# Expert stage: the weights of both layers as one record per page from HBM, instead of from SBUF by registers on TensorE and VectorE

## What is computed

```python
x = x + xattn(layernorm(x), ctx_1024, Wq, bq, Wk, bk, Wv, bv, Wo, bo)
n = layernorm(x)                                   # 16384 tokens x 256
e = argmax(n @ router_w.T + router_b, axis=-1)     # one of 32
h = relu(n @ weights1[e] + bias1[e])               # 256 -> 64
x = x + relu(h @ weights2[e] + bias2[e])           # 64 -> 256
```

## Time and profile before

| | before |
|---|---|
| median of 3 runs | 1328.94 us |
| profiled execution: span | 1326.5 us |
| profiled execution: what lies around the span | not shown; the median is 2.4 us above the span |
| PE busy / DVE / ACT / POOL | 87% / 71% / 63% / 64% |
| attention stage up to the table's load | about 0 to 1059 us |
| expert stage | 1059 to 1326.5 us |
| DMA in the expert stage (1100 to 1250 us) | share 0.54, 168 to 172 GB/s |

### The profile page before, as it was taken

One profiled execution on the slowest core, in us unless ns is written; L12 is line 12 of the kernel. 1 busy time (PEld: TensorE's weight loads), 2 busy tenths in 40 slices (PEclk: granted clock), 3 DMA queues, 4 the chain that ended last, 5 costly groups with the idle time before them and its releaser, 6 DMA issues.

```text
span 1326.5 us, 38982 instructions
## 1 busy us (share of the span) xinstructions
PE 1149.7 (87%) x15015; PEld 879.9 (66%) x15015; DVE 943.3 (71%) x2449; ACT 833.1 (63%) x1892; POOL 850.8 (64%) x1613
## 2 busy tenths in 40 slices
PE   4899999999999999999999999999986077777785
PEld 3677777777767777777777777777764066666664
DVE  4588788888778878788888778877775155555554
ACT  2577677777677777777777677777764044444443
POOL 4235677677776766777677776766744746666665
PEclk9899999999999999999999999999998589999999
DMA  8215222422222222222222222222101255555540
GB/s 253 89 58 113 66 74 66 131 81 70 73 83 69 66 73 66 66 74 66 67 81 70 73 83 70 66 74 58 34 27 39 92 169 175 169 163 181 161 120 19
DMA packets 89235, 120.37 MB, mean 91 GB/s; under 512 B 12176, under 2 KB 71963, under 8 KB 88861
## 3 DMA queue, kind: packets, MB, share of 16 engines
q1 hardware_dynamic: 75230, 84.03, 22.2%
q0 software_dynamic: 13824, 33.85, 7.0%
HBM read 60.61 MB, written 59.31 MB: 90 GB/s over the span
## 4 chain that ended last, share of the span: by engine, by line
PE 52%; DVE 32%; issue 7%; ACT 4%; POOL 2%; DVEq 1%; DMA 1%; another core or an unknown queue 0%; SPq 0%; POOLq 0%
DVE mx L565 14%; PE pB L787 11%; PE pA L740 9%; PE pB L794 5%; PE sc L747 4%; PE sc L942 4%; DVE tr L589 3%; PE m L950 3%; PE sc L769 3%; DVE nrm L593 3%; PE m L756 3%; DVE row L574 3%; PE sc L933 2%; PE sc L778 2%; PE pA L731 2%
## 5 line engine op out<-in xcount | busy, mean ns | idle before, releaser
L565 DVE TENSOR_REDUCE mx<-m 128x4 bf16<-128x512 f32 x512 | 324.0, 673 | 60.6 <-PE m L756 60.4
L446 ACT ACTIVATE arena<-sc 128x512 f32<-128x512 f32 x512 | 264.5, 604 | 33.9 <-PE sc L778 21.7
L397 POOL DMA_INDIRECT out<-arena x160 | 159.6, 997 | 104.7 <-DVE arena L706 69.0
L769 PE MATMUL sc<-qk 32*128 32x256 f32 x2048 | 167.0, 397 | 0.2
L368 POOL DMA_INDIRECT pages<-row,slot_i x128 | 131.9, 1030 | 49.3 <-issue 32.3
L787 PE MATMUL pB<-arena 128*32 128x128 f32 x4096 | 147.3, 276 | 14.3 <-issue 0.9
L589 DVE STREAM_TRANSPOSE tr<-pB 128x512 f32<-128x512 f32 x128 | 91.8, 717 | 82.6 <-PE pB L787 73.8
L524 ACT ACTIVATE arena<-sc 128x256 f32<-128x256 f32 x160 | 61.2, 383 | 135.4 <-PE sc L933 82.4
L794 PE MATMUL pB<-wo_s,aT 128*128 128x256 f32 x512 | 139.5, 396 | 3.9 <-DVE aT L598 3.9
L787 PEld LDWEIGHTS pB<-arena 128*32 128x32 f32 x4096 | 107.9, 110 | 37.4 <-DVE row L574 31.1
L276 POOL TENSOR_SCALAR row<-row 128x2 f32<-128x2 f32 x64 | 14.6, 228 | 161.4 <-ACT xn L430 161.4
(11 more groups left out here) (133 smaller groups left out, 2716.6 us busy)
## 6 DMA issues: line engine op xcount, KB each, us to landing
arena<-pages SPq DMA_DIRECT2D x40, 520.0 KB
xs<-x_in SPq DMA_DIRECT2D x128, 128.0 KB, 2.1
cT<-ctxT SPq DMA_DIRECT2D x64, 256.0 KB, 4.3
pages<-empty SPq DMA_DIRECT2D x120, 130.0 KB
pages<-empty SPq DMA_DIRECT2D x1, 5200.0 KB, 18.9
out<-arena POOLq DMA_INDIRECT x160
w2s<-w SPq DMA_DIRECT2D x1, 2080.0 KB
qk<-w SPq DMA_DIRECT2D x1, 2064.0 KB
```

Source lines behind the costliest of these rows:

```text
L397: pool.indirect_dma_start(out_rows, bass.IndirectOffsetOnAxis(pr[:, r, COL_TOKEN:COL_TOKEN + 1].bitcast(U32), 0), pr[:, r, 0:D], None, bou ...
L446: act.activation(pt[:, u % 2, g].rearrange("p i k -> p (i k)"), sc[g][:, :], ACT.Exp).then_inc(S["exp_out"], 1)
L565: ins = dve.tensor_reduce(mx[:, 32 * g:32 * g + 4], mb[i][:, :].rearrange("p (h k) -> p h k", h=4), AX.X, ALU.max)
L769: pe.matmul(dst, kT[rows, q % 2, c, u * P:(u + 1) * P], qM[rows, q % 2, :, c, u * P:(u + 1) * P], start=(c == 0), stop=False, skip_group_c ...
```

## The change

Both layers' weights of an expert become one record of 385 used columns (of a pitch of 388) times 128 partitions in a new HBM tensor `weights`: columns 0 to 128 hold the first layer and its bias, columns 129 to 384 the second layer with its bias row. The records are put together by three DMAs of SP in the attention stage, behind quads 5, 6 and 7. In the expert stage SP alone reads `table`, four values at a time, and issues for each page a DMA of 128 rows of 1540 bytes from `weights` at a register's offset into a ring `wt` of 12 (over the space of `qk`). The page loads keep their ring of 20, but each is now issued between the register loads and the weight loads of a group of four, two groups ahead. TensorE waits for the landing of a record (`w_in0` to `w_in11`) and takes both layers from the ring at fixed addresses. VectorE's copy, both engines' register loads, `w1s`, `w2s`, `w1p` and `w1_out` are gone.

```diff
-W1R = 5
-W1C = 192
+WR = 12
+WC = 388
...
+    W1E = 2 * HID + 1
+    W2E = W1E + D
+    weights = nc.dram_tensor("weights", (E, P, WC), F32).ap()
...
-        w2s = sb("w2s", [E, D])
-        w1s = qk[:, 0:E * (2 * HID + 1)].rearrange("p (e h) -> p e h", e=E)
+        wt = qk[:, 0:WR * WC].rearrange("p (n c) -> p n c", c=WC)
-        w1p = cT[:, :, :].rearrange("p c t -> p (c t)")[:, 0:W1R * W1C].rearrange("p (n c) -> p n c", c=W1C)
...
-                if q == 1:
-                    sp.dma_start(w2s[64:P, :, :], empty[64:P, 0:D].unsqueeze(1).to_broadcast([64, E, D])).then_inc(S["w2_zero"], 16)
                 if q == 5:
+                    sp.dma_start(weights.rearrange("e p c -> p e c")[64:P, :, W1E:W2E],
+                                 empty[64:P, 0:D].unsqueeze(1).to_broadcast([64, E, D])).then_inc(S["w2_zero"], 16)
+                if q == 6:
+                    sp.dma_start(weights.rearrange("e p c -> p e c")[:, :, 0:W1E], w1).then_inc(S["ld_w1"], 16)
+                if q == 7:
                     sp.wait_ge(S["w2_zero"], 16)
-                    sp.dma_start(w2s[0:HID + 1, :, :], w2).then_inc(S["ld_w2"], 16)
+                    sp.dma_start(weights.rearrange("e p c -> p e c")[0:HID + 1, :, W1E:W2E], w2).then_inc(S["ld_w2"], 16)
 
             after(sp, "T_done", 16, NQ - 1, 15)
-            sp.dma_start(w1s, w1).then_inc(S["ld_w1"], 16)
+            sp.wait_ge(S["ld_w1"], 16)
+            sp.wait_ge(S["ld_w2"], 16)
...
-            for n in range(0, PAGES, GP):
+
+            def load_pages(n):
                 g = n % RING // GP
                 if n >= RING:
                     sp.wait_ge(S[f"wrote{g}"], n // RING * (16 * GP))
                 sp.dma_start(pr[:, g * GP:(g + 1) * GP, :], page_view[:, n:n + GP, :]).then_inc(S[f"page_in{g}"], 16)
+
+            def load_weights(n, e):
+                if n >= WR:
+                    after(sp, "y_done", 1, n - WR, 0)
+                sp.dma_start(wt[:, n % WR, 0:W2E],
+                             weights[bass.ds(e, 1), :, 0:W2E].rearrange("e p c -> p (e c)")).then_inc(S[f"w_in{n % WR}"], 16)
+
+            load_pages(0)
+            load_pages(GP)
+            sp.wait_ge(S["table_in"], 16)
+            for n in range(0, PAGES, AT_ONCE):
+                _, experts = nc.values_load_multi_w_load_instructions(table[0:1, n:n + AT_ONCE], engines=(mybir.EngineType.SP,), min_val=0, max_val=E - 1)
+                if n + 2 * GP < PAGES:
+                    load_pages(n + 2 * GP)
+                for k in range(AT_ONCE):
+                    load_weights(n + k, experts[k])
...
             def h_copy(n):
                 after(act, "h_done", 1, n, 0)
                 act.activation(hT[0:HID, n % DEEP, :], sc[2 + n % 2][0:HID, 0:P], ACT.Relu,
-                               bias=w1p[0:HID, n % W1R, 2 * HID:2 * HID + 1]).then_inc(S["h_out"], 1)
+                               bias=wt[0:HID, n % WR, 2 * HID:2 * HID + 1]).then_inc(S["h_out"], 1)
...
-                if n >= W1R:
-                    after(dve, "h_out", 1, n - W1R, 0)
-                dve.tensor_copy(w1p[:, n % W1R, 0:2 * HID + 1], w1s[:, bass.ds(e, 1), :].rearrange("p e h -> p (e h)")).then_inc(S["w1_out"], 1)
...
-            after(dve, "ctx_out", 1, NQ - 1, 0)
-            dve.memset(w1p[:, :, 2 * HID + 1:W1C], 0.0)
...
-            dve.wait_ge(S["ld_w1"], 16)
-            dve.wait_ge(S["table_in"], 16)
...
-                        _, experts = nc.values_load_multi_w_load_instructions(table[0:1, n:n + AT_ONCE], engines=(mybir.EngineType.DVE,), min_val=0, max_val=E - 1)
-                    page_norm(n, experts[n % AT_ONCE])
+                    page_norm(n)
...
             def page_first(n):
-                after(pe, "w1_out", 1, n, 0)
+                pe.wait_ge(S[f"w_in{n % WR}"], n // WR * 16 + 16)
...
-                    ins = pe.matmul(sc[2 + n % 2][:, 0:P], w1p[:, n % W1R, i * HID:i * HID + P],
+                    ins = pe.matmul(sc[2 + n % 2][:, 0:P], wt[:, n % WR, i * HID:i * HID + P],
...
-                pe.matmul(mid[n % 4][:, 0:D], hT[:, n % DEEP, :], w2s[:, bass.ds(e, 1), :].rearrange("p e d -> p (e d)"),
+                pe.matmul(mid[n % 4][:, 0:D], hT[:, n % DEEP, :], wt[:, n % WR, W1E:W2E],
...
-            pe.wait_ge(S["ld_w2"], 16)
-            pe.wait_ge(S["table_in"], 16)
...
-                        _, experts = nc.values_load_multi_w_load_instructions(table[0:1, n - 4:n - 4 + AT_ONCE], engines=(mybir.EngineType.PE,), min_val=0, max_val=E - 1)
-                    page_second(n - 4, experts[n % AT_ONCE])
+                    page_second(n - 4)
```

More of the change, by code:

```diff
@@ L152, in build @@
           noff_out step_out fresh_slots all_slots grew_out shift_out nxt_old room_out nxt_out own_slots slot_int
+          w_in0 w_in1 w_in2 w_in3 w_in4 w_in5 w_in6 w_in7 w_in8 w_in9 w_in10 w_in11
           scattered table_in page_in0 page_in1 page_in2 page_in3 page_in4 wrote0 wrote1 wrote2 wrote3 wrote4
-          w1_out pn_out pT_done h_done y_done pT_out h_out po_out""".split()
+          pn_out pT_done h_done y_done pT_out h_out po_out""".split()
         names += [f"ld_x{k}_{u}" for k in range(4) for u in range(QB)]
@@ L689, in _, with page_norm @@
                             scan(s - 2)
-            def page_norm(n, e):
+            def page_norm(n):
                 r = n % RING
-                if n >= W1R:
-                    after(dve, "h_out", 1, n - W1R, 0)
-                dve.tensor_copy(w1p[:, n % W1R, 0:2 * HID + 1], w1s[:, bass.ds(e, 1), :].rearrange("p e h -> p (e h)")).then_inc(S["w1_out"], 1)
                 if r % GP == 0:
@@ L708, in _ @@
             mid = [mb[0], mb[1], pA, pB]
-            after(dve, "ctx_out", 1, NQ - 1, 0)
-            dve.memset(w1p[:, :, 2 * HID + 1:W1C], 0.0)
             dve.tensor_copy(hT[64:P, :, :].rearrange("p n t -> p (n t)"),
                             cst[64:P, C_ONE:C_ONE + 1].to_broadcast([64, DEEP * P])).then_inc(S["ex_init"], 1)
-            dve.wait_ge(S["ld_w1"], 16)
-            dve.wait_ge(S["table_in"], 16)
             for n in range(PAGES + LAG):
                 if n < PAGES:
-                    if n % AT_ONCE == 0:
-                        _, experts = nc.values_load_multi_w_load_instructions(table[0:1, n:n + AT_ONCE], engines=(mybir.EngineType.DVE,), min_val=0, max_val=E - 1)
-                    page_norm(n, experts[n % AT_ONCE])
+                    page_norm(n)
                 if n >= LAG:
@@ L941, in page_first, with page_second @@
                 for i in range(2):
-                    ins = pe.matmul(sc[2 + n % 2][:, 0:P], w1p[:, n % W1R, i * HID:i * HID + P],
+                    ins = pe.matmul(sc[2 + n % 2][:, 0:P], wt[:, n % WR, i * HID:i * HID + P],
                                     pnT[:, n % DEEP, i * P:(i + 1) * P], start=(i == 0), stop=(i == 1))
                 ins.then_inc(S["h_done"], 1)
-            def page_second(n, e):
+            def page_second(n):
                 if n >= 4:
```

## The result

The changed kernel takes 1344.36 us (1343.04 to 1347.07, 4 runs) against 1327.72 us of before (4 runs): ratio 1.0108, interval 1.0076 to 1.0140. It is slower, by 17 us from median to median and by 14 us by the ratio; the forecast was 1306 us, 23 us faster than the 1328.94 us that were known then. The profiled execution has a span of 1341.1 us.

The account below looks back on a forecast made before the run. It took TensorE's and VectorE's in-order pace with registers as the present bound, and the page-to-record loop as the next. Expert stage 245.3 to 217.2 us, saving 28.1, less 1.2 and 4, gave 1306 us, range 1284 to 1336.

Parts of the forecast that it names:

- (a): Expert-stage loop, from end of a page's second layer to SP's page load: 3.85 us, bounds 3.5 and 5.
- the way round from a page written to a record used: Expert-stage loop: record n cannot be requested before page n-9 is written; 11.2 us for two groups, chance 0.42.
- the last of the three signs of being wrong: Expert stage: the prediction is wrong if the scatters' landing stretches by more than 0.3 us.
- (b): Expert-stage loop, from SP's page-load issue to the landing of record n: 5.2 us, bounds 4.6 and 6.5.
- The holes and their worth: TensorE's idle times per group, from register reads and late transposes: 1.9 us a group, 74 us if nothing took over.
- DMA bandwidth: Expert stage: 461 KB a page at 363 GB/s takes 1.27 us, 5.1 us a group.
- (c): Expert-stage loop, from the start of `page_first(n)` to the end of the second layer of page n-1: 2.14 us.
- SP at nothing: SP's register block and issues in the expert stage: 3.0 to 4.6 us a group, costed at nothing.
- Start: Start of the expert stage: `page_first(0)` begins at about 1066.8 instead of 1065.59, 1.2 us lost.
- Late landings: Expert stage: landings 1.2 to 1.6 us late, no longer absorbed by the page ring; 4 us, bounds nothing and 8.
- The slower one: Expert-stage loop with writes and records queueing, slower from 12.3 us on; 1351 us at 13.6; chance 0.18.
- Every record pays a whole start of its own: Expert-stage records one after another: 3.1 us each, 12.4 a group, about 1570 us; chance 0.01.

Follow-up runs that it names:

- run 1: Changed kernel with the four record issues of a group put ahead of its page load: 1279.48 us, ratio 0.9662 to the kernel before.
- run 2: Changed kernel with page loads issued one group ahead instead of two: 1280.70 us, ratio 0.9692 to the kernel before.
- run 5: Changed kernel with page loads issued three groups ahead instead of two: 1533.86 us, ratio 1.1453 to the kernel before.
- run 4: Kernel before plus 160 DMAs of record size into a spare ring that no engine waits for: 1326.34 us, ratio 1.0034.
- Run 12: Kernel before with the expert taken as n mod 32, so TensorE and VectorE read no registers, on a third chip: 1277.97 us, ratio 0.9662.
- run 11: Changed kernel with page loads one group ahead instead of two, repeated on a third chip: 1283.20 us, ratio 0.9691 to the kernel before.
- run 10: The changed kernel itself, measured again on a third chip: 1334.51 us, ratio 1.0075 to the kernel before.
- runs 9 and 10: Kernel before, unchanged, and the changed kernel, both measured again on a third chip: 1324.08 us and 1334.51 us.
- runs 5 to 8: Four on one chip: run 5; changed kernel, one group ahead with short records, 0.9980; run 7; kernel before, fixed experts for TensorE alone, 1.0003.
- run 7: Kernel before with the expert taken as n mod 32, so TensorE and VectorE read no registers: 1332.73 us, ratio 0.9960.

## Why the prediction was wrong

The step that failed is (a): "3.55 us, and 0.3 for writes that now share the engines". The bound that was named, the way round from a page written to a record used, is the right one: turning two issues round (run 1) or asking for an older page (run 2) spreads it over three groups and gains 3%, a round over one group (run 5) nearly doubles the stage, and the traffic without the dependence (run 4) costs 0.3%. What was mis-sized is, above all, one term of its sum. The sharing of the engines lengthened the scatter's leg by 2.1 us (4.60 against 2.52 on the same chip) where I gave it 0.3, and (a) came to 5.7 for 3.85, over my upper bound of 5: 1.85 of the 2.25 us by which the round was too short. It is the last of the three signs of being wrong that the prediction names. I had given the scatters' delay of the *record* 0.6 us in (b) and that was right (5.12 for 5.2); the same reasoning the other way, a scatter of 131 KB among four records of 197 KB and a page group of 532 KB on the other queue, was not made.

Point by point:

- *The holes and their worth.* Right in sum. Run 12 shows 47 us without registers, POOL's pace as the floor. How it splits between TensorE's hole and VectorE's no run shows.
- *DMA bandwidth, 363 GB/s.* Right; run 11 reaches 361.
- *(b), page load to `page_first`.* Right, 5.12.
- *(c), 2.14.* 2.65. In 26 of the 34 rounds of run 10 it is 2.24; in the other 8 the matmuls ran in part at TensorE's lower clock, and it is 3.97. The second record of a group is not the reason: TensorE waits for it in 2 of the 34 rounds. The lower clock after a wait, 0.4 us a round on average, was left out.
- *The sum.* 19 rounds of 13.45 for 11.2 are 43 us; 28 forecast as saved less 43 is 15 lost, and 39 x (6.53 - 6.19) = 13 were measured between runs 9 and 10.
- *SP at nothing.* Right: it sat waiting 2.7 us before each page load (run 10). Its register block took 0.30 + 4 x (0.15 + 0.02) = 0.98 us, a record's issue 0.33 with 0.07 for its offset.
- *Start, 1.2 us.* From the first page load to `page_first(0)` it is 7.5 us, on the same chip 6.4 before: 1.1.
- *Late landings, 4 us.* Not seen as a term of its own: the leg is 4.6 us on average and varies from 2.4 to 5.8. It was the tail of the same thing that (a) got wrong, and I had priced it apart.
- *Staging.* Right at nothing. The w1 copy landed in 20.4 us, the zero fill in 16.0.
- *The rivals.* The slower one is what happened, by its own mechanism, at 13.5 where it gave 12.3 as the point from which it decides. Its sentence "nothing in the trace shows both queues full at once" was the warning: with the bound at nine tenths of the DMA engines, an upper bound of (a) 1.15 us above the chosen value was too narrow, and 0.18 too little. *Every record pays a whole start of its own*, the case of the rule of at least 1 MiB per DMA in the Trainium skill (DMA: Bandwidth & Descriptors, "Rules for kernel authors"), did not hold: records of 197 KB, together with page loads and scatters, ran at 361 GB/s (run 11). The fixed 2 us, which the prediction takes from the section "Anatomy of one DMA" of the same page of the Trainium skill, are told there of DMAs that GpSimd issues, and SP issues the records. These landed 4.3 us after their issue (median, run 10) while the next ones were already under way.

TensorE's clock in such a round, timeline of the changed kernel in run 10:

```profile
1163.27 0.97 PE L956 MATMUL sc<-arena,qk 128*128 128x128 f32 x4 [2.29 <-DMA qk<-weights]
...
1165.32 1.06 PE L956 MATMUL sc<-arena,qk 128*128 128x128 f32 x4
...
1167.23 0.61 PE L956 MATMUL sc<-arena,qk 128*128 128x128 f32 x4
```

After a wait of 2.3 us the same four matmuls take 0.97 and 1.06 us, and two pages later 0.61: the lower and the upper of its two levels (1.2 and 2.4 GHz). The granted clock is 0.60 from 1163 to 1166 us and 1.00 from 1168 to 1172. In the two windows from 1100 to 1200 us it is 0.98 and 0.87, for 1.00 before. Not every wait does it: in run 10 TensorE comes back at the lower clock in 6 of 34 rounds and falls to it right behind in 2. The Trainium skill (TensorE: Matmul & The Clock Gate, section "HAM oscillation — how this bites in real kernels") tells of a kernel that waits for a DMA at each tile and starts each one at the lower clock; this trace agrees for those 8 rounds of 34, not for the rest. In them the wait that the records brought costs twice, and that is most of what (c) has too much.

## What to carry to other kernels

In an in-order DMA queue, a load that waits for a buffer to be written out holds back everything issued behind it: count the pages from the awaited write to the use of the next load as a loop, and put the load that TensorE needs soonest ahead of the one that can wait, or ask for an older buffer. Size that loop with the landing times of the load that will be there, not with those of the quiet trace: from half-full to full engines the landing of a scatter doubled. Here one page load, issued behind the four records of its group instead of in front of them, turns a change that loses 1% into one that wins 3%.

## What the runs showed that was not expected

**Late signals on some chips.** On the chip of runs 5 to 8, in the timeline of run 7, TensorE's transposes end at 1181.25 + 0.38 = 1181.63 by their record, ScalarE is free at 1182.29, and it starts at 1183.40:

```profile
1181.25 0.38 PE L931 MATMUL sc<-cst,arena 128*128 128x128 f32 x2
1181.93 0.36 ACT L528 ACTIVATE arena<-sc,cT 64x128 f32<-64x128 f32 x1 [1.11 <-PE sc L940]
...
1182.43 0.68 PE L940 MATMUL sc<-arena,cT 128*128 128x128 f32 x4 [0.80 <-ACT arena L528]
...
1183.40 0.38 ACT L524 ACTIVATE arena<-sc 128x256 f32<-128x256 f32 x1 [1.11 <-remote]
...
1184.86 0.36 ACT L528 ACTIVATE arena<-sc,cT 64x128 f32<-64x128 f32 x1 [1.07 <-remote]
1184.90 0.42 DVE L706 SCALAR_TENSOR_TENSOR arena<-m,arena 128x256 f32<-128x256 f32 x1 [2.03 <-PE m L948]
```

Three starts in a row, 1.46 us apart, each 1.07 to 1.11 us after ScalarE's idle began. VectorE is held too, for 2.03 us until 1184.90. Where a trace has 61 to 72 such late starts in the stage (together 81 to 95 us, partly hidden), the gain is gone that the kernel has elsewhere: no registers has the ratio 0.9960 there and 0.9662 on the third chip. The first trace of before has 10 of them, that of the changed kernel 45 (46 us in sum); eight traces on two other chips have none. So it goes with the chip, or with the moment, which these runs do not tell apart, and it is seen more where TensorE runs at its dense pace of 1.10 us a page. The granted clock does not show it: in run 7 it is 1.00 at that place, and the last drop before it is at 1167 to 1171. What it is stays open; that TensorE's real ends lag the modelled ones is the nearest reading, and no run tried it.

**The loop is still there in the kernel that wins.** With one group more in the loop the leg is longer (5.36 us) than where it hurt (4.60), and the round is too, 15.4 us for 13.45. TensorE still waits for a record in nearly every group, in run 11 from 1080 to 1240 us:

```profile
PEld sc L955 <- DMA qk<-weights: 22.8, 29, 2.0
```

But the round is spread over three groups, 5.1 us each, and that is POOL's pace, four scatters of 1.28. The length of a landing says nothing without the number of pages that it is spread over.
